# Second attention of a five-layer kernel: unmasked keys transposed, state grown on 64 rows, recall ahead of growth, first projections in the drain in front

## The reference

```python
sq, sk = elu(q) + 1, elu(k) + 1
out_m = einsum('bhsd,mhde->mbhse', sq, memories)          # 4 memories
rel   = einsum('bhsd,mhd->mbhs', sq, memory_norms)
out_m = out_m / clip(rel, EPS, None)[..., None]
weights = softmax(rel.mean(axis=-1), axis=0)
mem_out = einsum('mbhse,mbh->bhse', out_m, weights)
kv_cum, k_cum = cumsum(sk (x) v), cumsum(sk)              # over the sequence
local = (sq . kv_cum) / clip(sq . k_cum, EPS, None)[..., None]
out = (g * mem_out + (1 - g) * local) @ w_o.T
```

## Time and profile before

| what | value |
|---|---|
| median of three runs | 2572.85 us |
| the profiled execution | 2570.97 us |
| its span | 2568.9 us |
| granted TensorE clock, mean of the span | 0.986 |
| instructions | 78013 |

### The profile page before, as it was taken

How to read it: one execution, slowest core, us unless ns; L and a number is a source line. 1 busy time by engine, 2 the same in 40 slices (tenths; PEclk the granted TensorE clock), 3 DMA queues, 4 the chain that set the end, 5 groups by cost and what they waited for, 6 DMA issues and landing times.

```text
span 2568.9 us, 78013 instructions
## 1 busy us (share of the span) xinstructions
PE 2442.4 (95%) x32232; PEld 2131.2 (83%) x32232; DVE 1842.7 (72%) x4308; ACT 1420.4 (55%) x2361; POOL 1285.9 (50%) x1398
## 2 busy tenths in 40 slices
PE   4999999999999989999999999989999999979999
PEld 3888888888888868888888899878888888858998
DVE  8999899577777789999985766545655565646665
ACT  4555555533334335556665888754544444418886
POOL 5878888621112138889996333213434443453331
PEclk9999999999999999999999999999999999979999
DMA  5000000000000010000000000000000000000111
GB/s 188 1 7 1 1 1 1 1 23 22 24 23 24 23 49 1 1 1 1 1 1 1 18 1 1 1 20 18 18 18 16 17 18 17 18 3 26 34 34 42
DMA packets 67566, 45.97 MB, mean 18 GB/s; under 512 B 13184, under 2 KB 66192, under 8 KB 67216
## 3 DMA queue, kind: packets, MB, share of 16 engines
q1 hardware_dynamic: 67216, 41.00, 5.7%
HBM read 15.78 MB, written 8.40 MB: 9 GB/s over the span
## 4 chain that ended last, share of the span: by engine, by line
PE 69%; issue 14%; POOL 11%; DVE 5%; ACT 2%; DMA 0%; SPq 0%; POOLq 0%; DVEq 0%; ACTq 0%
PE ps L46 11%; PE ps L48 11%; PE ps L47 11%; PE ps L1527 5%; PE ps L1525 5%; PE ps L1506 5%; PE ps L1505 5%; PE ps L612 3%; PE ps L264 3%; PE ps L1172 3%; PE ps L1099 2%; POOL a1pry L2081 2%; POOL a1pry L2083 2%; POOL a1l L2069 2%; PE ps L1130 2%
## 5 line engine op out<-in xcount | busy, mean ns | idle before, releaser
L1570 DVE TENSOR_TENSOR gHl<-gHf,gHh 128x512 fp32r<-128x512 f32 x256 | 186.6, 729 | 184.3 <-ACT gHh L1546 184.1
L231 POOL TENSOR_SCALAR ve<-mv 128x4 f32<-128x4 f32 x96 | 22.2, 231 | 584.4 <-DVE mv L221 580.2
L46 PE MATMUL ps<-WGH,XTH 128*128 128x512 f32 (+1 forms) x768 | 299.6, 390 | 7.3 <-ACT fSG L681 4.4
L48 PE MATMUL ps<-WGL,XTH 128*128 128x512 f32 (+1 forms) x768 | 290.2, 378 | 0.0
L47 PE MATMUL ps<-WGH,XTL 128*128 128x512 f32 (+1 forms) x768 | 289.5, 377 | 0.0
L681 ACT ACTIVATE fSG<-ps 128x704 f32<-128x704 f32 x128 | 97.1, 759 | 312.2 <-PE ps L48 312.2
L827 POOL TENSOR_TENSOR fHTL<-fHTF,fHTH 128x768 fp32r<-128x768 f32 x128 | 236.2, 1845 | 62.2 <-ACT fHTF L690 62.2
L1525 PE MATMUL ps<-W2T,gHh 128*128 128x256 f32 x1024 | 255.4, 283 | 0.0
L1527 PE MATMUL ps<-W2T,gHl 128*128 128x256 f32 x1024 | 253.0, 281 | 0.0
L2069 POOL TENSOR_TENSOR a1l<-a1l,a1rc 128x128 f32<-128x128 f32 x128 | 49.7, 409 | 358.4 <-DVE a1rc L2036 358.4
L46 PE MATMUL ps<-WDH,fHTH 128*128 128x256 f32 x768 | 221.8, 289 | 2.8 <-issue 2.8
(11 more groups left out here) (240 smaller groups left out, 7103.4 us busy)
## 6 DMA issues: line engine op xcount, KB each, us to landing
X<-in_x SPq DMA_DIRECT2D x16, 512.0 KB, 8.8
a0vp<-a0vt SPq DMA_DIRECT2D x256, 32.0 KB, 1.9
a1vp<-a1vk SPq DMA_DIRECT2D x256, 32.0 KB, 2.1
out<-X SPq DMA_DIRECT2D x16, 512.0 KB, 2.9
tws<-in_w SPq DMA_DIRECT2D x2, 1024.0 KB, 7.7
WN<-in_wgu SPq DMA_DIRECT2D x3, 384.0 KB, 5.0
a0km<-in_wqkv SPq DMA_DIRECT2D x2, 384.0 KB, 3.3
a1pry<-in_aw SPq DMA_DIRECT2D x1, 768.0 KB, 4.6
```

Source lines behind the costliest of these rows:

```text
L46: e.matmul(o, hh, mh, start=first, stop=False)
L48: return e.matmul(o, hh, ml, start=False, stop=last)
L1570: dve.tensor_tensor(Hl[m % 8][:, :], Hf[m % 4][:, :], Hh[m % 8][:, :].bitcast(F32), ALU.subtract).then_inc(s_hl, 1)
```

## The change

- The transposes take the unmasked keys SK, now in two buffers, two transposes per tile instead of four, and no longer wait for `keys`; the scores do.
- Growth multiplies 64 rows (tokens) of keys with the same 64 rows of VK1 (values and a block of ones) instead of 128 rows of masked keys with VP1. What belongs to other heads is taken out by a multiply with the constant tile `own` when VectorE reads the state. The wait for VP1's DMAs moves from `grow` to `values`.
- ScalarE's copy to VK1 has 512 columns instead of 768. The state buffers are three instead of four.
- `recall(r)` stands behind `values_keys(n)` and ahead of `grow(m, 0)`, and VectorE's recall multiplies ahead of the states and masks; the ring's order follows. POOL does its sums over the memories ahead of the rescaling.
- The first two projections are issued between the last units of `ffn1`.

```diff
-        SK = sb(a1, "a1sk", [P, 2, 512])
+        SK = [sb(a1, f"a1sk{i}", [P, 2, 512]) for i in range(2)]
...
-        VK1 = [sb(a1, f"a1vk{i}", [P, 768]) for i in range(2)]
+        VK1 = [sb(a1, f"a1vk{i}", [P, 544]) for i in range(2)]
...
+        own = sb(a1w, "a1own", [P, 2, 36])
...
+                for k in range(2):
+                    for b in range(2):
+                        dve.tensor_copy(own[:, k, 16 * b:16 * b + 16], par[:, b:b + 1].broadcast_to([P, 16]))
+                        dve.tensor_copy(own[:, k, 32 + 2 * k + b:33 + 2 * k + b], par[:, b:b + 1])
...
         def ffn1_pe(pe, S):
             for m in range(7 if S == 3 else 0, 8 * NS + LAG):
                 ffn1_unit(pe, S, m)
+                if S == 3 and m == 8 * NS - 1:
+                    attn1_ready(pe)
+                    attn1_proj(pe, 0, 0)
+                if S == 3 and m == 8 * NS + 1:
+                    pe.wait_ge(s_ge, 8 * NS)
+                    attn1_proj(pe, 0, 1)
...
-            yield from [("p", 0, 0), ("p", 0, 1)]
+            yield from [("p", 0, 1), ("p", 0, 0)]
             for n in range(NT + FAR + 1):
                 i, j = n // 4 + 1, n % 4
                 if n < NT:
-                    yield from [("v", n), ("s", n, 0), ("s", n, 1)]
-                far = [("m", n - FAR, 0), ("m", n - FAR, 1)] if 0 <= n - FAR < NT else []
-                yield from [("l", n), *far] if n < NT else [*far, ("l", n)]
+                    yield ("v", n)
+                if 0 <= n - FAR < NT:
+                    yield from [("m", n - FAR, 0), ("m", n - FAR, 1)]
+                if n < NT:
+                    yield from [("s", n, 0), ("s", n, 1)]
+                yield ("l", n)
...
-                    sp.wait_ge(n_up, after1(2 * (n - 2) + 1))
...
                         sp.dma_start(VP1[n % 2][64 * m:64 * m + 64, h, 128 * m:128 * m + 128],
-                                     VK1[n % 2][64 * h:64 * h + 64, 128 * m:128 * m + 128]).then_inc(d_v1[n % 2], 16)
+                                     VK1[n % 2][64 * h:64 * h + 64, 256 + 128 * m:384 + 128 * m]).then_inc(d_v1[n % 2], 16)
...
                 if j == 0:
-                    pe.wait_ge(n_km, i + 1)
-                for h in range(2):
-                    for k in range(2):
-                        c = 256 + 256 * h + 128 * k
-                        ks = slice(256 * j + 128 * h, 256 * j + 128 * h + 128)
-                        t = pe.transpose(bank[:, c:c + 128], KM1[i % 2][:, k, ks], ident[:, :])
+                    pe.wait_ge(n_el, 4 * i + 4)
+                for k in range(2):
+                    t = pe.transpose(bank[:, 128 * k:128 * k + 128], SK[i % 2][:, k, ts], ident[:, :])
...
-                pe.wait_ge(d_v1[m % 2], 64 * (m // 2) + 64)
...
-                        t = pe.matmul(PS[7][32 * q:32 * q + 32, 36 * k:36 * k + 36], VK1[m % 2][:, c:c + 32],
-                                      VP1[m % 2][:, h, 4 * k + q:288:8], start=(j % 16 == 0 and k == 0), stop=True,
+                        t = pe.matmul(PS[7][32 * q:32 * q + 32, 36 * k:36 * k + 36], VK1[m % 2][rows, c:c + 32],
+                                      VK1[m % 2][rows, 256 + 4 * k + q:544:8], start=(j % 16 == 0 and k == 0), stop=True,
                                       skip_group_check=True)
...
                 pe.wait_ge(n_am, 2 * m + 2)
+                pe.wait_ge(d_v1[m % 2], 64 * (m // 2) + 64)
...
                 if j == 0:
-                    pe.wait_ge(n_el, 4 * i + 2)
+                    pe.wait_ge(n_km, i + 1)
...
-            act.wait_ge(s_d1, 8 * NS)
+            act.wait_ge(s_d1, 8 * NS - 6)
             proj(0, 0)
             proj(0, 1)
+            act.wait_ge(s_d1, 8 * NS)
             keys(0)
...
-                    act.activation(VK1[n % 2][:, :], pair1("v", n)[:, 0:768], ACT.Copy).then_inc(n_vke, 1)
+                    act.activation(VK1[n % 2][:, 0:512], pair1("v", n)[:, 0:512], ACT.Copy).then_inc(n_vke, 1)
...
-                    dve.tensor_copy(a1S[j % 4][:, :, 0:36],
-                                    PS[7][:, 0:72].rearrange("p (k v) -> p k v", k=2)).then_inc(n_ss, 1)
+                    dve.tensor_tensor(a1S[j % 3][:, :, 0:36], PS[7][:, 0:72].rearrange("p (k v) -> p k v", k=2),
+                                      own[:, :, :], ALU.mult).then_inc(n_ss, 1)
```

More of the change, by code:

```diff
@@ L154, in macaron @@
         a1YT = [sb(a1, f"a1YT{i}", [P, D]) for i in range(2)]
-        VP1 = [sb(a1, f"a1vp{i}", [P, 2, 288]) for i in range(2)]
+        VP1 = [sb(a1, f"a1vp{i}", [P, 2, 256]) for i in range(2)]
         CF = [sb(a1, f"a1cf{i}", [P, 64]) for i in range(2)]
@@ L159, in macaron @@
         S0 = sb(a1, "a1s0", [P, 2, 64])
-        a1S = [sb(a1, f"a1S{i}", [P, 2, 64]) for i in range(4)]
+        a1S = [sb(a1, f"a1S{i}", [P, 2, 64]) for i in range(3)]
         PRY = sb(a1, "a1pry", [P, 1536])
@@ L1429, in attn1_set_dve @@
                 dve.wait_ge(s_on, 1)
+                dve.memset(own[:, :, :], 0.0)
                 for b in range(2):
@@ L1468, in attn1_set_pool @@
                 pool.memset(v[:, :, :], 0.0)
+            for v in VK1:
+                pool.memset(v[:, 512:544], 1.0)
             pool.memset(ON[:, :, :], 0.0).then_inc(s_v1z, 1)
@@ L1472, in attn1_set_pool @@
                 for b in range(2):
[L1473 to L1477, removed]
+                    t = pool.memset(ON[64 * b:64 * b + 64, k, 2 * k + b:2 * k + b + 1], 1.0)
             t.then_inc(s_v1z, 1)
@@ L1674, in attn1_sp, with attn1_take, attn1_proj @@
                         sp.dma_start(VP1[n % 2][64 * m:64 * m + 64, h, 128 * m:128 * m + 128],
-                                     VK1[n % 2][64 * h:64 * h + 64, 128 * m:128 * m + 128]).then_inc(d_v1[n % 2], 16)
-        def attn1_pe(pe):
[L1678 to L1683, removed]
+                                     VK1[n % 2][64 * h:64 * h + 64, 256 + 128 * m:384 + 128 * m]).then_inc(d_v1[n % 2], 16)
+        def attn1_take(pe, *name):
+            at = ring1[name]
+            if at >= 3:
+                for s, v in emptied1(*order1[at - 3]):
+                    pe.wait_ge(s, v)
+            return pair1(*name)
+        def attn1_proj(pe, i, g):
+            F = 64 + i
+            bank = attn1_take(pe, "p", i, g)
+            pe.wait_ge(s_xl, 2 * F + 2)
+            for c in range(2):
+                o = 2 * g + c
+                sl = slice(128 * o, 128 * o + 128)
+                for k in range(2):
+                    t = mm3(pe, bank[:, 512 * c:512 * c + 512], a1WH[:, k, sl], a1WL[:, k, sl],
+                            XTH[F % 2][:, k, :], XTL[F % 2][:, k, :], k == 0, k == 1)
+                t.then_inc(n_pj, 1)
+        def attn1_pe(pe):
             def turn_x(i):
-                bank = take("t", i)
+                bank = attn1_take(pe, "t", i)
                 pe.wait_ge(s_xn, 64 + i + 1)
@@ L1707, in values_keys @@
                 ts = slice(128 * j, 128 * j + 128)
-                bank = take("v", n)
+                bank = attn1_take(pe, "v", n)
                 for k in range(2):
-                    mm3(pe, bank[:, 0:256], XTH[F % 2][:, k, ts], XTL[F % 2][:, k, ts],
+                    mm3(pe, bank[:, 256:512], XTH[F % 2][:, k, ts], XTL[F % 2][:, k, ts],
                         a1WH[:, k, 512:768], a1WL[:, k, 512:768], k == 0, k == 1)
                 if j == 0:
-                    pe.wait_ge(n_km, i + 1)
-                for h in range(2):
-                    for k in range(2):
-                        c = 256 + 256 * h + 128 * k
-                        ks = slice(256 * j + 128 * h, 256 * j + 128 * h + 128)
-                        t = pe.transpose(bank[:, c:c + 128], KM1[i % 2][:, k, ks], ident[:, :])
+                    pe.wait_ge(n_el, 4 * i + 4)
+                for k in range(2):
+                    t = pe.transpose(bank[:, 128 * k:128 * k + 128], SK[i % 2][:, k, ts], ident[:, :])
                 t.then_inc(n_vk, 1)
@@ L1759, in scores @@
                 if j == 0:
-                    pe.wait_ge(n_el, 4 * i + 2)
-                banks = [take("s", n, g) for g in range(2)]
+                    pe.wait_ge(n_km, i + 1)
+                banks = [attn1_take(pe, "s", n, g) for g in range(2)]
                 for h in range(2):
@@ L1778, in enter @@
                     j = 2 * m + h
[L1779 removed]
+                    s = a1S[(j - 1) % 3] if j % 16 else S0
                     if j % 16:
@@ L1798, in recall @@
                 tq = slice(128 * (r % 4), 128 * (r % 4) + 128)
-                banks = [take("m", r, g) for g in range(2)]
+                banks = [attn1_take(pe, "m", r, g) for g in range(2)]
                 for k in range(2):
@@ L1817, in attn1_pe @@
                     pe.wait_ge(s_xd, 64 * 3 + 64)
+                if 0 <= r < NT:
+                    recall(r)
                 if 0 <= m < NT:
@@ L1825, in attn1_pe @@
                     enter(m)
-                if n >= NT and r < NT:
-                    recall(r)
-                bank = take("l", n)
+                bank = attn1_take(pe, "l", n)
```

(26 more changed lines are left out.)

40 lines of the change are left out of this document (7 added, 33 removed).

## The result

| | before | after |
|---|---|---|
| median of the runs beside each other | 2572.63 us | 2623.02 us |
| lowest to highest | 2569.93 to 2576.93 | 2619.61 to 2630.04 |
| the profiled execution, its span | 2570.97, 2568.9 us | 2619.61, 2617.7 us |
| granted clock, mean of the span | 0.986 | 0.988 |

The ratio of after to before is 1.0198, with a 95% interval of 1.0172 to 1.0224: slower by 50.4 us. The forecast was 2616 with a range of 2580 to 2640.

The account below looks back on a forecast made before the run. PE was taken as the bound, busy 95% of the span. Added 73.4 us less removed 28.1 gives net +45.3 on the profiled 2570.97: 2616 us, range 2580 to 2640.

Parts of the forecast that it names:

- (a): Key transposes on PE: two of four go, 0.22 us per tile in 60 tiles, 13.2 us removed.
- (b): PE's wait for masked keys ahead of the transposes: 10.0 of 10.6 us go.
- (k): Items taken at nothing, among them ACT's smaller copy and PE's wait for the DMAs, moved to values and covered.
- (d): At n = 64, recall no longer behind growth and values, and PE's wait for POOL's sums goes: 2.0 us removed.
- (e): Recall waits for VectorE's X addition to free its PSUM pair: 0.79 in 18 tiles, 1.05 in 13; 14.2 plus 13.7 us.
- (g): Second growth waits for the state behind VectorE's recall multiplies: 17.3 us in 48 tiles, 6.2 more in 7 softmax tiles.
- (h): 64-row growth on PE: matmul time unchanged, but a change of form costs 0.13 once per tile, 8.3 us.
- (j): First projections moved into the drain ahead of the stage: later elus and masking delay the first scores, 0.7 us added.
- half hidden: Rival: PE's own hiccups fall into the new waits, so 36.7 of 73.4 us goes: 2580 us, chance 0.12.
- VectorE clears in time: Rival: VectorE reaches X addition and state before PE needs them, leaving removals, switches and front: 2552 us, chance 0.12.
- The clock falls: Rival: gaps in PE's work lower its granted clock for a twentieth of the stage, about 28 us more: 2644, chance 0.06.
- 64 rows cost double: Rival: growth on 64 rows takes twice as long, adding 15 us, within the range; no separate chance given.

Follow-up runs that it names:

- the order back: Kernel after with the order of before on PE, ring, VectorE and POOL (recall behind the Y transposes), rest kept: 2564.93 us, ratio 0.9972.
- the X addition ahead: Kernel after with VectorE's X addition moved between the second elu's halves, or ahead of the low parts of turned x: 2595.56 us, ratio 1.0097.
- the first state ahead: Kernel after with VectorE's first state eviction moved ahead of softmax, coefficients and recall multiplies: 2613.24 us, ratio 1.0163.
- the kernel with 128 rows: The order back, but each half-growth takes all 128 rows instead of 64: 2555.78 us, ratio 0.9946.
- the order alone: Kernel before with only the new order (recall ahead of growth); four masked transposes, 128-row growth, projections not moved: 2630.66 us, ratio 1.0227.
- three moves: Kernel after with the first state ahead, the X addition ahead, and ACT's YT copy ahead of L's: 2584.27 us, ratio 1.0062.

## Why the prediction was right

It was right in sign and in mechanism, and 7.0 below the median. Its net sum of 45.3 stands against 46.4 in the stage of the profiled execution. That the two are so close is in part luck: the sum had no term for the 11 us that the order gives back between PE's steps, nor for the stops that grew by about as much. By its own terms:

- **(a), (b) Transposes and masked keys, -23.2.** The wait is gone. The two transposes take 0.31 from their start to growth's where four took 0.53. At n = 4 and 8 the gain was 2.6 and 3.0 for a predicted 2.0 and the transposes' 0.22; tile 9 gave back 1.0, by the wait for VP1's DMAs (k). The kernel with the order back checks these terms: -13.2 - 10.0 + 8.3 + 0.7, and 7.3 for the second change of form (56 second growths), which no wait covers there, is -6.9; -6.6 was measured.
- **(c) The old wait for the state, -2.9.** Not separately tested.
- **(d) The tail, -2.0.** The wait for POOL's sums at n = 64 is gone in after, and the part from tile 63 on is 3.6 shorter. That doesn't size the term: the five kernels with PE's order of after take 318.7 to 321.0 there, the order back 320.4, before 322.6. No run separates it.
- **(e) Recall behind X, 27.9.** 0.79 and 1.00 for 0.79 and 1.05. Putting the X addition ahead took 27.5 off the kernel, 17.3 of it ahead of recall by the starts, so the reader of that bank is what held recall.
- **(f) The out-projection behind YT, 13.0.** 0.81 for 0.81.
- **(g) The second growth behind the state, 17.3, and the softmax tiles, 6.2.** 2.41 after recall for 2.42 at the usual tile. In the softmax tiles it starts 3.36 after recall for a predicted 3.30. VectorE sets that moment, which is why it fits; PE's own way there took 0.66 for recall and not 0.73, and 1.11 for values and sums and not 0.95, so that it waited 0.27 and not 0.36. Putting the first state ahead took 9.8 off the kernel, and the scores got part of the rest.
- **(h) The change of form, 8.3.** 0.38 to 0.39 in place of 0.26 in the traces, and 9.2 for both changes by the kernel with 128 rows. Counted by tiles both changes would give about 120 x 0.13 = 15.6, less some 4 of waits for the state that come back with 128 rows (6.5 against 2.3 from 1690 to 2250). The last 2 us may be stops, 15.6 against 13.1 inside groups of equal matmuls, which is not shown.
- **(i) The state multiply.** 0.22 for 0.21.
- **(j) The front, 0.7.** Too small: tiles 0 and 1 took 1.4 more than before (19.78 against 18.40), and the move alone costs 2.2. Tile 0 by itself is a poor measure: the kernel before takes 10.00 for it and the order alone, whose program is the same up to there, 8.92.
- **(k) At nothing.** The prediction said that without cover the landing of VP1's DMAs would show as a wait of values. It did, once, 1.15 at tile 9.

Of the order as a whole the prediction's terms make 52.2 (45.3 against the -6.9 above), and 57.0 to 58.1 was measured. In tiles 10 to 62 the waits come to 56, less about 11 between the steps, plus some 11.5, of which 9.0 are stops inside groups of equal matmuls (22.1 in after, 13.1 with the order back). The prediction had such stops help, under "half hidden". There was more of them, on top of the waits.

The rivals: *half the waits hidden* fell, since each wait has its full size in the timeline. *VectorE clears in time* fell: X ends 1.84 after v behind a projection (2038.10 + 0.41 less 2036.67), where 1.05 was the point of decision. Moving the addition ahead, to an end at 1.30, came nearest (2015.83 + 0.41 less 2014.94), and even with three moves the kernel stays slower than before. *The clock falls* fell: 1.00 from 1950 to 2150 at 89% busy, and 0.98 at the lowest in any of the stretches of 100 us from 1750 to 2150. The tail had 0.84 in the stretch shown; in the one that matches rows 2, 2307 to 2357, it had 0.77 for 0.69 before. *64 rows cost double* fell by the kernel with 128 rows.

Two expectations of the experiments were off by more than the forecast of the change: the order alone was dearer by 10, and the X addition ahead gained twice what was said. Each was costed as a sum of single waits. Neither sum had a term for the stops of PE without a releaser, 12.6 more than before in the first and 6.5 less than after in the second, and the second took its waits from the brackets.

## What to carry to other kernels

Moving a PE step forward in a tile is priced by who reads the banks it takes, and by what now stands ahead of the next steps on the readers' engines. Trace each bank's last reader on the timeline, and add 0.15 us for the release. If the reader's end comes after the moment when PE wants the bank, the difference is paid in every tile, though the reader's engine is idle for over 40% of the stage, as VectorE was here. A split of a contraction into half the rows saved no PE time here, as the number of matmuls stayed, and cost 0.13 us at each change of form.

## What was not expected of the hardware

PE sometimes stops in the middle of a group of equal matmuls, with no releaser in the profile. In after:

```profile
2114.58 0.44 PE L1742 MATMUL ps<-a1vk 64*32 64x36 f32 x12 [0.19 <-DVE a1S L1969]
2115.99 0.30 PE L1742 MATMUL ps<-a1vk 64*32 64x36 f32 x4 [0.97 <-issue]
```

Twelve of sixteen matmuls run, then nothing for 0.97 us, then the other four. The order alone had 1.06 of it in the middle of the scores. From 1750 to 2240 such idle time sums to 3.3 us before (longest 0.5), 5.1 with the order back, 7.2 with the X addition ahead, 8.6 with growth on 128 rows and 9.3 after (longest 1.1). The brackets understate it. Where a distance between neighbouring starts in one group is more than 0.08 above its median over all nine kernels, the excess sums in tiles 10 to 62 to 7.4 before, 13.1 with the order back, 15.6 with growth on 128 rows and with the X addition ahead, 20.0 with the order alone, 22.1 after and 29.6 with the first state ahead.

The place of a stop is set by the program. Four kernels have PE's program of after, and all four stop in this group behind the twelfth matmul. With the X addition ahead:

```profile
2098.33 0.44 PE L1742 MATMUL ps<-a1vk 64*32 64x36 f32 x12 [0.19 <-DVE a1S L1976]
2099.47 0.30 PE L1742 MATMUL ps<-a1vk 64*32 64x36 f32 x4 [0.70 <-issue]
```

Count the instructions of TensorE in the trace, its matmuls, weight loads and semaphore instructions together, from the first one on. Of the 208 stops inside groups that are longer than 0.2 us, in tiles 10 to 62 of the nine kernels, 197 lie at the same place modulo 256 (192 to 194). The profile's list of DMA queues, after, has one queue with as many packets as TensorE has blocks of 256 instructions (its 65736 recorded ones make 256.8):

```profile
q8 instruction: 257, 4.21, 0.7%
```

Its packets (16384 bytes each) take about 1 us. Their times in the traces, from 1750 to 2240, tell the stops apart. All 184 stops of more than 0.2 us at that place (give or take one instruction), in nine kernels, end 1.1 to 1.6 us after the end of such a packet; the one above ends 1.40 after it, the same one with the X addition ahead 1.30. The other 588 times that a group crosses the place, without such a stop, the last packet ended 3.5 us before by the median (105 of them lie between 1.1 and 1.6 too). That fits a PE that stands there until its next instructions have come. It is read from times alone, and no run varied it. Why a packet comes late, and why the new order has more such stops than the old, is open.
